# A two-turn hardware loop and its register waits written out as constants, on five engines of one core

## The chip, the cores and the metric

The kernel runs on one core of a Trainium2 chip. The metric is the device time of one execution in microseconds (us); the median of several runs is compared. Engines are named as in the profile: PE is TensorE's matmuls (PEld its weight loads), DVE is VectorE, ACT is ScalarE, POOL is GpSimd, SP is SyncE, which only issues DMAs here. "SPq", "DVEq" and the like are what an engine's sequencer does by itself.

## The reference

The input x has 2048 tokens of 128 values. A recurrent mixer comes first, then a transformer of two layers with local attention over windows of 64 tokens.

```python
x = x + _layernorm(mixer(_layernorm(x)))                 # gated scan over the 2048 tokens
x = x + _layernorm(ffn(_layernorm(x)))                   # ffn: two of the layers below, B, N = (2, 1024)

def _layer(x, ...):
    h = shift_token(x)                                   # half of the features come from the token before
    q, k, v = split(h @ wqkv, 3)                         # 8 heads of 64
    q, k = rotary_xpos(l2norm(q) * qs, l2norm(k) * ksc)
    o = local_attention(q, k, v)                         # window of 64, looks one window back
    x = x + o @ wo
    h = layernorm(shift_token(x)) * lg + lb
    a, g = split(h @ w1 + b1, 2)
    return x + (a * gelu(g)) @ w2 + b2
```

## The kernel before

Tokens are worked on in tiles of 128, four tiles to a group (`GT = 4`, `GROUPS = 4`); the two layers run one after the other over the same 16 tiles, so there are 32 tiles and `LAST = 8` groups. After the mixer each engine runs a sequence of passes. Pass `G` has four steps `j`; in step `j` the engine works on several tiles at different stages (`cur`, `prev`, `mid`, `done`, `after` are the tiles `4G + j + 3 - back`). In a pass with G >= 1 the feed-forward of group `G - 1` runs at `j = 2`, after its layer norm at `j = 1`.

There is no planner. The order on each engine is that of the program text, and engines meet by counting semaphores: `wait_ge(s, n)` holds the engine until semaphore `s` has reached `n`, and an operation's `then_inc` raises it at its end.

`passes` (L262) writes the passes -1 and 0 out with G as a Python number. Then a loop on each engine (`Fori`) runs G = 1 and 2 with G in a register. The passes 3 and 4, then 5 and 6, then a half pass 7 and `ending` are written out again. Inside the loop a semaphore value such as `32 * G` is computed in registers, and so are some addresses: the DMAs of `tables`, `head_scales` and `group_in` on SP and the columns of `low_half` on POOL. SP has one more loop (L418), over the groups 1 and 2 of the mixer's result.

`settle` (L237) raises a semaphore that nobody waits for. It stands behind certain waits, in passes that are written out as well: in `variances` (DVE, L1164 and L1168), `norm_roots` (POOL, L504), behind `h2_ready` (POOL, L540), before the carry copy (POOL, L561), in `scores` (PE, L697), in `mix_values` (PE, L722) and twice in `feed_forward` (PE, L756 and L761); on SP (L235) only behind waits on a register.

What the steps below speak of, by line: `act_t_lo` (L1140, `split_inputs`, once a pass at `j = 0`) follows ScalarE's `act_t_hi` (L888) and TensorE's transposes of `h_tok` (L641). L541, L542, L505, L507 and L552 are POOL's work for one tile (rotary sums, roots of the norms, scaling); L494 scales the tables of the next group. `low_half` (L482) is done by POOL in the loop's two turns, after the tile of `j = 2`; it prepares half of the second layer's weights each time. L590 to L594 project q, k and v, L701 and L708 make the scores, L726 mixes the values. `y` (L1236) is the group's result and the copy of `x_early` (L1229) follows it on DVE. `variances` is called 12 times: for `h2` in the passes 1 to 7 and once in `ending`, for `y` in the passes 5 and 6 and twice in `ending`. It consists of four `bn_stats` (L1166), a wait for them, and four `bn_aggr` (L1170). L1034 is the same `bn_aggr` in the mixer phase, where no `settle` stands before it.

Of the kernel before, what the change touches and what calls it, by code (L numbers as in the profile page):

```python
# [24 lines left out]
GT = 4  # L25
# [10 lines left out]


CHAIN = {0: 5, 1: 6}
# [29 lines left out]
def sandwich_kernel(nc, x, w_hg_t, w_out_t, wqkv, wo, ln_g, ln_b, w1, b1, w2, b2,  # L68
                    tables, head_scales, consts, out):
    ctx = ExitStack()  # L70
    with ctx:
# [13 lines left out]
        def group_tiles(ap, g):  # L85

            return ap[:, GT * g:GT * g + GT, :] if isinstance(g, int) else ap[:, bass.ds(GT * g, GT), :]
# [137 lines left out]
        settled = {e.name: sem(f"settled_{e.name}") for e in (mybir.EngineType.SP, mybir.EngineType.DVE, mybir.EngineType.Pool, mybir.EngineType.PE)}  # L225
# [15 lines left out]

        class At:

            def __init__(self, G, j, back, layer):
# [3 lines left out]
                if isinstance(self.t, int):  # L252
                    self.valid = 0 <= self.t < DEPTH * TILES
                    self.layer = self.t // TILES
                    self.first = self.t % TILES == 0
                else:
                    self.valid, self.layer, self.first = True, layer, False

        def tile(t):
            return At(t // GT, t % GT, 3, DEPTH - 1)  # L260

        def passes(eng, body, ending, steps=None):  # L262

            body(-1, 0)
            body(0, 0)
            for layer in range(DEPTH - 1):
                G0, G1 = GROUPS * layer + 1, GROUPS * (layer + 1) - 1
                if steps:
                    steps.enter()
                with eng.Fori(G0, G1) as G:  # L270
                    if steps:
                        steps.at(G - G0, CHAIN[layer])
                    body(G, layer)
                if steps:
                    steps.leave(G1 - G0)
                body(G1, layer)
                body(G1 + 1, layer)
            for G in range(GROUPS * (DEPTH - 1) + 1, LAST - 1):
                body(G, DEPTH - 1)
            body(LAST - 1, DEPTH - 1, 2)  # L280
            ending()

        class Steps:


            def __init__(self, eng, s):
                self.eng, self.sem, self.base, self.n = eng, s, 0, 0
# [5 lines left out]
            def catch_up(self):  # L293

                self.eng.wait_ge(self.sem, self.base + self.n)
# [4 lines left out]

            def enter(self):
                self.start, self.n = self.base + self.n, 0

            def at(self, i, each):
                self.base, self.each = self.start + i * each, each

            def leave(self, times):
                assert self.n == self.each, f"a pass of the loop has {self.n} steps"
                self.base, self.n = self.start + times * self.each, 0
# [9 lines left out]
        def _(sp):  # L319
# [35 lines left out]
            def load_tables(G):  # L355
# [3 lines left out]
                sp.dma_start(head_scale[:, :], head_scales[G:G + 1].broadcast_to([P, TABW]) if isinstance(G, int)  # L359
                             else head_scales[bass.ds(G, 1), :].broadcast_to([P, TABW])).then_inc(tab_in, 16)  # L360
# [6 lines left out]
            def load_h2(F):  # L367
# [3 lines left out]
                if isinstance(F, int) and F == LAST - 1:  # L371
# [10 lines left out]
            def load_carry(F):  # L382

                need(sp, h2_in, 64 * (F + 1))
                ends = isinstance(F, int) and F % GROUPS == GROUPS - 1
                last = zeros[P - 1:P, 64:128] if ends else x_attn[P - 1:P, GT, 64:128]
                dst = x_last if isinstance(F, int) and F == LAST - 2 else x_attn
                sp.dma_start(dst[P - 1:P, 0, 64:128], last).then_inc(carry_in, 16)

            def store(F, layer):  # L390
                if layer == 0:
# [3 lines left out]
                    if not (isinstance(F, int) and F == GROUPS - 1):  # L395
# [4 lines left out]
                if not (isinstance(F, int) and F == LAST - 1):  # L400
                    need(sp, carry_in, 16 * (F + 1))


            def store_mixed(g):
                sp.dma_start(tiles_of(group_in[g, 1:1 + GTOK, :]), group_tiles(normed, g)).then_inc(xf_stored, 16)
                if not (isinstance(g, int) and g == GROUPS - 1):
# [18 lines left out]
            def body(G, layer, count=GT):  # L425
                number = isinstance(G, int)
                for j in range(count):
                    cur = At(G, j, 0, layer)
                    if j == 0 and not (number and not 0 <= G < LAST - 1):
                        load_tables(G + 1)  # L430

                        if layer == 0 or (number and G <= GROUPS):
# [4 lines left out]
                    ffn = j == 0 and not (number and G < 1)  # L437
                    if ffn:
                        load_h2(G - 1)
                    if cur.valid and not (number and cur.t < GT):  # L440
# [9 lines left out]
                    if j == 3 and number and G > GROUPS + 1:  # L450
                        store(G - 2, DEPTH - 1)
                if count == GT and not (number and (G < 1 or G > GROUPS)):
                    store(G - 1, (G - 1) // GROUPS if number else layer)
# [7 lines left out]
            passes(sp, body, ending)  # L461
# [908 lines left out]
```

## Time and profile before

| | us |
|---|---|
| runs | 435.87, 436.12, 433.83; median 435.87 |
| span of the profiled execution, from the first to the last instruction | 431.7 |
| median of the runs less that span | 4.2 |
| PE busy | 351.5 (81% of the span) |
| DVE busy | 321.6 (74%) |
| POOL busy | 301.1 (70%) |
| PEld busy | 287.5 (67%) |
| ACT busy | 280.8 (65%) |

The profile is one execution. The profiled execution's own time is not given apart from its span; the median stands for it. Busy times of one engine's instructions overlap somewhat, as they are pipelined, and the ends of matmuls are modelled. The mean granted TensorE clock is 0.941 of full speed.

### The profile page before, as it was taken

To read this page: it belongs to the slowest core of one execution; us is meant where nothing else is said; L and a number is where in the kernel's file an instruction comes from. 1 tells how busy PE (TensorE), PEld (TensorE's weight loads), DVE (VectorE), ACT (ScalarE), POOL (GpSimd) and SP (SyncE) were. 2 spreads that over 40 slices of the span, in tenths; PEclk is the share of its full clock that TensorE was granted. 3 is DMA by queue.
4 is the path that set the end of the run, shared out by engine and by line. 5 is a ranking of instruction groups with operands and counts; after the bars stand their busy time and mean duration, and the time that the engine had idled before them with its cause. 6 is when DMAs were issued, how large, how long until landed. Compare 5 with 4: busy or idle time off the path is not lost.

```text
span 431.7 us, 11030 instructions
## 1 busy us (share of the span) xinstructions
PE 351.5 (81%) x3832; PEld 287.5 (67%) x3832; DVE 321.6 (74%) x751; ACT 280.8 (65%) x844; POOL 301.1 (70%) x247
## 2 busy tenths in 40 slices
PE   1573055899999899999999999999999989988781
PEld 1352034677778687778777887788778867766561
DVE  6889964787689767966796788688869877954653
ACT  3552263688678677867786788678777868764430
POOL 2200419899999889988998699869887988780222
PEclk9996557999999999999999999999999999998966
DMA  7700042412142125112511342043204220220110
GB/s 262 225 0 0 13 125 60 110 27 50 46 118 56 32 55 141 30 30 64 133 32 33 105 94 51 15 121 76 62 3 117 65 53 2 57 57 2 24 49 25
DMA packets 42373, 28.29 MB, mean 66 GB/s; under 512 B 21668, under 2 KB 36566, under 8 KB 42326
## 3 DMA queue, kind: packets, MB, share of 16 engines
q1 hardware_dynamic: 42325, 27.68, 24.4%
q8 instruction: 27, 0.44, 0.4%
q14 instruction: 21, 0.16, 0.1%
HBM read 13.51 MB, written 3.15 MB: 39 GB/s over the span
## 4 chain that ended last, share of the span: by engine, by line
PE 37%; DVE 23%; POOL 19%; issue 11%; ACT 7%; DMA 1%; SPq 1%; POOLq 1%; DVEq 0%; ACTq 0%
POOL rn L507 7%; PE bank L726 5%; POOL rot L552 4%; PE bank L771 4%; DVE rot_sin L1153 4%; PE upper L708 3%; DVE rot_cos L1153 3%; POOL rot L541 3%; ACT probs L902 3%; PE bank L650 2%; PE bank L763 2%; DVE normed L1052 2%; PE upper L659 2%; PE bank L590 2%; DVE neg_max L1201 2%
## 5 line engine op out<-in xcount | busy, mean ns | idle before, releaser
L902 ACT ACTIVATE probs<-upper,neg_max 128x128 f32<-128x128 f32 x256 | 90.4, 369 | 48.5 <-DVE neg_max L1201 48.4
L507 POOL TENSOR_TENSOR rn<-floored,minus_half 128x16 f32<-128x16 f32 x32 | 93.8, 2930 | 2.7
L541 POOL TENSOR_TENSOR rot<-rot_cos,rot_sin 128x512 f32<-128x512 f32 x32 | 40.9, 1277 | 44.3 <-issue 23.6
L1201 DVE TENSOR_REDUCE neg_max<-upper 128x4 f32<-128x512 f32 x64 | 43.1, 684 | 27.5 <-PE upper L708 27.4
L552 POOL TENSOR_TENSOR rot<-rot,rn 128x1024 f32<-128x1024 f32 x32 | 60.9, 1903 | 2.5
L902 ACT ACTIVATION_READ_ACCUMULATOR probs<-upper,neg_max 128x1 f32 x256 | 53.0, 207 | 0.0
L590 PE MATMUL bank<-wqkv_hi,act_t_hi 128*128 128x512 f32 x96 | 43.3, 452 | 7.9 <-DVE act_t_lo L1140 2.8
L1153 DVE TENSOR_TENSOR rot_cos<-bank,tab 128x512 f32<-128x512 f32 x64 | 43.6, 681 | 2.0 <-PE bank L594 1.9
L1153 DVE TENSOR_TENSOR rot_sin<-bank,tab 128x512 f32<-128x512 f32 x64 | 43.4, 679 | 0.0
L542 POOL TENSOR_TENSOR rot<-rot_cos,rot_sin 128x512 f32<-128x512 f32 x32 | 40.9, 1279 | 0.0
L1160 DVE TENSOR_REDUCE ss<-sq 128x16 f32<-128x1024 f32 x32 | 38.7, 1209 | 2.4 <-ACT sq L944 2.3
L681 PE MATMUL upper<-const,probs 128*128 128x128 f32 x256 | 34.6, 275 | 5.4 <-ACT probs L902 5.3
L944 ACT ACTIVATE sq<-bank 128x512 f32<-128x512 f32 x64 | 36.9, 614 | 3.2 <-DVE rot_sin L1153 3.2
L591 PE MATMUL bank<-wqkv_hi,act_t_lo 128*128 128x512 f32 x96 | 38.6, 402 | 0.0
L594 PE MATMUL bank<-wqkv_lo,act_t_hi 128*128 128x512 f32 x96 | 38.6, 402 | 0.0
L726 PE MATMUL bank<-v_mid,probs_t 128*64 128x64 f32 x512 | 37.5, 228 | 0.9 <-ACT probs_t L909 0.6
L726 PEld LDWEIGHTS bank<-v_mid,probs_t 128*64 128x64 f32 x512 | 33.0, 140 | 7.0 <-issue 4.8
L726 PE MATMUL bank<-v_tok,probs_t 128*64 128x64 f32 x512 | 37.5, 228 | 0.0
L687 PEld LDWEIGHTS upper<-wo_sb,o_t 128*128 128x128 f32 x256 | 33.5, 193 | 3.4 <-ACT o_t L914 0.6
L687 PE MATMUL upper<-wo_sb,o_t 128*128 128x128 f32 x256 | 34.2, 277 | 0.2 <-ACT o_t L914 0.2
L708 PE MATMUL upper<-k_t,q_t 64*64 64x128 f32 x1024 | 34.3, 274 | 0.0
L590 PEld LDWEIGHTS bank<-wqkv_hi,act_t_hi 128*128 128x128 f32 x96 | 18.5, 192 | 23.1 <-issue 18.0
(140 smaller groups left out, 863.7 us busy)
## 6 DMA issues: line engine op xcount, KB each, us to landing
v_mid<-v_tok SPq DMA_DIRECT2D x64, 128.0 KB, 2.3
tab_raw<-tables SPq DMA_DIRECT2D x8, 512.0 KB, 3.4
h_tok<-group_in SPq DMA_DIRECT2D x14, 128.0 KB, 3.5
x_res<-group_in SPq DMA_DIRECT2D x28, 64.0 KB, 1.8
wqkv_raw<-wqkv SPq DMA_DIRECT2D x2, 768.0 KB, 6.8
x_in<-x SPq DMA_DIRECT2D x4, 256.0 KB, 3.6
head_scale<-head_scales SPq DMA_DIRECT2D x8, 128.0 KB, 4.0
group_in<-normed SPq DMA_DIRECT2D x4, 256.0 KB
```

Source lines behind the costliest of these rows:

```text
L507: pool.tensor_tensor(rn[:, 0:2 * HEADS], floored[:, 0:2 * HEADS], minus_half[:, :], ALU.pow).then_inc(rn_ready, 1)
L541: pool.tensor_tensor(rot[cur.par][:, :, 0:32], rot_cos[:, :, 0:32], rot_sin[:, :, 32:64], ALU.add).then_inc(rot_added, 1)
L542: pool.tensor_tensor(rot[cur.par][:, :, 32:64], rot_cos[:, :, 32:64], rot_sin[:, :, 0:32], ALU.add).then_inc(rot_added, 1)
L552: pool.tensor_tensor(rot[cur.par][:, :, :], rot[cur.par][:, :, :], rn[:, 0:2 * HEADS].unsqueeze(2).broadcast_to([P, 2 * HEADS, DH]), ALU.m ...
L590: pe.matmul(out_ap, lhs, rhs, start=True, stop=False)
L687: last = pe.matmul(to[:, 0:DIM], o_t[:, c, :], wo_sb[a.layer][:, c, :], start=(c == 0), stop=(c == 3))
L708: last = pe.matmul(s_bank[half][low:low + 64, p * P:(p + 1) * P], q_t[rows, p, low:low + 64], k_t[rows, p, at:at + P], start=False, stop=T ...
L726: last = pe.matmul(o_bank[low:low + 64, cols], probs_t[:, h, low:low + 64], v[:, cols], start=True, stop=True)
L902: last = act.activation(probs[:, h, :], s_bank[half][:, (h % 4) * P:(h % 4 + 1) * P], ACT.Exp, bias=neg_max[a.par][:, h:h + 1], accum_out= ...
L1153: dve.tensor_tensor(dst[:, n * HEADS:(n + 1) * HEADS, :], src, table.unsqueeze(1).broadcast_to([P, HEADS, DH]), ALU.mult).then_inc(done, 1)
L1160: dve.tensor_reduce(ss[:, :], sq[:, :].rearrange("p (h d) -> p h d", h=2 * HEADS), AX.X, ALU.add).then_inc(ss_ready, 1)
L1201: dve.tensor_reduce(neg_max[a.par][:, 4 * half:4 * half + 4], src, AX.X, ALU.max, negate=True).then_inc(max_ready, 1)
```

## The change

All passes from -1 to 6 and the half pass 7 are written out with G as a number, so the loop, the registers, the loop's own chain count (`Steps.enter`, `at`, `leave`) and every `isinstance` branch go. Every `settle` goes, with its semaphores. SP's loop over the mixer's groups is written out. `low_half` is done where G is 1 or 2. No operation, transfer, buffer or order is changed otherwise.

```diff
-        settled = {e.name: sem(f"settled_{e.name}") for e in (mybir.EngineType.SP, mybir.EngineType.DVE, mybir.EngineType.Pool, mybir.EngineType.PE)}
         def need(eng, s, value):
-            if isinstance(value, int) and value <= 0:
-                return
-            eng.wait_ge(s, value)
-            if eng.engine == mybir.EngineType.SP and not isinstance(value, int):
-                settle(eng)
-
-        def settle(eng):
-            eng.sem_inc(settled[eng.engine.name], 1)
+            if value > 0:
+                eng.wait_ge(s, value)
...
-        def passes(eng, body, ending, steps=None):
-            body(-1, 0)
-            body(0, 0)
-            for layer in range(DEPTH - 1):
-                G0, G1 = GROUPS * layer + 1, GROUPS * (layer + 1) - 1
-                if steps:
-                    steps.enter()
-                with eng.Fori(G0, G1) as G:
-                    if steps:
-                        steps.at(G - G0, CHAIN[layer])
-                    body(G, layer)
-                if steps:
-                    steps.leave(G1 - G0)
-                body(G1, layer)
-                body(G1 + 1, layer)
-            for G in range(GROUPS * (DEPTH - 1) + 1, LAST - 1):
-                body(G, DEPTH - 1)
-            body(LAST - 1, DEPTH - 1, 2)
+        def passes(body, ending):
+            for G in range(-1, LAST - 1):
+                body(G)
+            body(LAST - 1, 2)
             ending()
...
-            with sp.Fori(1, GROUPS - 1) as g:
-                need(sp, xf_ready, g + 1)
+            for g in range(1, GROUPS - 1):
+                sp.wait_ge(xf_ready, g + 1)
                 store_mixed(g)
...
-                    cols = bass.ds(G * n - n, n)
+                    cols = slice(G * n - n, G * n)
...
                 pool.wait_ge(ss_ready, t + 1)
-                settle(pool)
...
-                        if j == 2 and not (number and G < 1):
+                        if j == 2 and G >= 1:
                             pool.wait_ge(h2_ready, G)
-                            settle(pool)
...
-                    if not number and layer == 0 and j == 2:
+                    if G in (1, 2) and j == 2:
                         low_half(G)
...
                 need(pe, pt_saved1, a.t)
-                settle(pe)
...
                     if h == PAIRS:
                         pe.wait_ge(pt_saved1, a.t + 1)
-                        settle(pe)
...
                     if c == 0:
                         pe.wait_ge(h2_split, F + 1)
-                        settle(pe)
...
             def variances(src, done, at=0):
-                settle(dve)
                 for k in range(GT):
                     last = dve.bn_stats(stats[:, k, :], src[:, k, :])
                 link(last)
-                settle(dve)
                 for k in range(GT):
                     last = dve.bn_aggr(mean_var[:, at + k, :], stats[:, k, :])
                 last.then_inc(done, 1)
```

## Rows read from the trace of the kernel before

**Rows 1.** The page: chain of work that ended last, shares by engine.
```profile
PE 37%; DVE 23%; POOL 19%; issue 11%; ACT 7%; DMA 1%; SPq 1%; POOLq 1%; DVEq 0%; ACTq 0%
```
**Rows 2.** Table of stretches: length, busy us of each engine (instructions), clock, DMA share.
```profile
127.21:169.81 42.60, 40.08 (x479) 33.47 (x475) 32.83 (x63) 32.31 (x100) 37.84 (x30) 1.00 0.26 66
169.81:212.24 42.43, 39.83 (x474) 33.31 (x470) 32.83 (x64) 32.31 (x100) 37.66 (x30) 1.00 0.26 66
212.24:254.20 41.96, 40.07 (x481) 33.36 (x474) 32.72 (x63) 32.27 (x100) 34.76 (x28) 1.00 0.27 68
254.20:296.27 42.07, 40.08 (x482) 33.38 (x474) 32.86 (x63) 32.28 (x100) 34.99 (x28) 1.00 0.26 67
```
**Rows 3.** Timeline of VectorE: start, us, instruction, idle time before and its releaser.
```profile
161.14 0.69 DVE L1201 TENSOR_REDUCE neg_max<-upper 128x4 f32<-128x512 f32 x1 [2.04 <-PE upper L708]
...
196.12 0.69 DVE L1236 TENSOR_TENSOR y<-bank,x_attn 128x512 f32<-128x512 f32 x1 [1.35 <-PE bank L771]
196.84 0.54 DVE L1229 COPY x_attn<-x_early 128x256 f32<-128x256 f32 x1
...
238.28 0.69 DVE L1236 TENSOR_TENSOR y<-bank,x_attn 128x512 f32<-128x512 f32 x1 [1.25 <-PE bank L771]
239.01 0.29 DVE L1229 COPY x_attn<-x_early 128x256 f32<-128x256 f32 x1
...
245.75 0.69 DVE L1201 TENSOR_REDUCE neg_max<-upper 128x4 f32<-128x512 f32 x1 [1.81 <-PE upper L708]
```
**Rows 4.** Timeline of GpSimd.
```profile
195.40 1.83 POOL L482 TENSOR_TENSOR wqkv_lo<-wqkv_raw,wqkv_hi  x1
...
241.86 1.29 POOL L541 TENSOR_TENSOR rot<-rot_cos,rot_sin 128x512 f32<-128x512 f32 x1 [4.16 <-issue]
```
**Rows 5.** Chain that ended last, start, us, what: loop's second turn, then pass 3.
```profile
167.31 1.08 PE bank L726 x32
168.39 0.60 PE bank L641 x4
...
169.10 0.59 ACT act_t_hi L888
...
169.81 0.70 DVE act_t_lo L1140
...
211.00 0.59 PE bank L641 x4
```
**Rows 6.** Timelines of ScalarE and VectorE, pass 3.
```profile
211.62 0.58 ACT L888 CAST act_t_hi<-bank 128x512 fp32r<-128x512 f32 x1 [0.87 <-PE bank L641]
...
212.24 0.69 DVE L1140 TENSOR_TENSOR act_t_lo<-bank,act_t_hi 128x512 fp32r<-128x512 f32 x1 [2.15 <-ACT act_t_hi L888]
```
**Rows 7.** VectorE's groups by line: busy us, mean ns, idle us before, releaser.
```profile
L1170 DVE BATCH_NORM_AGGREGATE mean_var<-stats 128x2 f32<-128x6 f32 x48 | 4.8, 159 | 2.1 <-DVE stats L1166 1.8
...
L1034 DVE BATCH_NORM_AGGREGATE mean_var<-stats 128x2 f32<-128x6 f32 x48 | 3.7, 151 | 0.1
```
**Rows 8.** Timeline of VectorE: the first tile's sum of squares, the last `y`.
```profile
64.24 1.22 DVE L1160 TENSOR_REDUCE ss<-sq 128x16 f32<-128x1024 f32 x1 [1.60 <-ACT sq L944]
...
423.36 0.87 DVE L1166 BATCH_NORM_STATS2 stats<-y 128x6 f32<-128x128 f32 x4 [0.16 <-DVE y L1236]
```
**Rows 9.** Timeline of GpSimd, first tile.
```profile
65.67 0.25 POOL L505 TENSOR_SCALAR floored<-ss 128x16 f32<-128x16 f32 x1 [0.36 <-DVE ss L1160]
```
**Rows 10.** Chain that ended last, pass 3.
```profile
243.40 1.08 PE bank L726 x32
244.48 0.34 PE upper L701 x4
```
**Rows 11.** TensorE's groups by line.
```profile
L726 PE MATMUL bank<-v_mid,probs_t 128*64 128x64 f32 x512 | 37.5, 228 | 0.9 <-ACT probs_t L909 0.6
```
**Rows 12.** The page: DMA queue (packets, MB, share), DMA issues (KB, us to landing).
```profile
q8 instruction: 27, 0.44, 0.4%
...
v_mid<-v_tok SPq DMA_DIRECT2D x64, 128.0 KB, 2.3
```

More of the change, by code:

```diff
@@ L35 @@
 RSQRT_SEED = 0x5F3759DF
-CHAIN = {0: 5, 1: 6}
 def rotary_tables():
@@ L299, in link @@
                 self.catch_up()
[L301 to L309, printed above, removed]
         def low_pieces(l):
@@ L399, in store @@
                     sp.dma_start(by_group(out)[F - GROUPS], y_out[:, :, :]).then_inc(stored, 16)
-                if not (isinstance(F, int) and F == LAST - 1):
+                if not (F == LAST - 1):
                     need(sp, carry_in, 16 * (F + 1))
@@ L449, in body @@
                         load_carry(G - 1)
-                    if j == 3 and number and G > GROUPS + 1:
+                    if j == 3 and G > GROUPS + 1:
                         store(G - 2, DEPTH - 1)
-                if count == GT and not (number and (G < 1 or G > GROUPS)):
-                    store(G - 1, (G - 1) // GROUPS if number else layer)
+                if count == GT and 1 <= G <= GROUPS:
+                    store(G - 1, (G - 1) // GROUPS)
             def ending():
@@ L736, in feed_forward @@
             def feed_forward(F, layer, t_now, between=None):
-                taken = min(t_now, DEPTH * TILES) if isinstance(F, int) else t_now
+                taken = min(t_now, DEPTH * TILES)
                 pe.wait_ge(h2t_saved, 2 * F + 1)
@@ L780, in _, with body @@
             transpose_inputs(0)
-            def body(G, layer, count=GT):
-                number = isinstance(G, int)
-                if number and G == GROUPS - 1:
+            def body(G, count=GT):
+                if G == GROUPS - 1:
                     pe.wait_ge(w_high, 2 * DEPTH)
@@ L787, in body @@
                 for j in range(count):
-                    cur, prev, mid, done, after = (At(G, j, back, layer) for back in range(5))
-                    ffn = j == 2 and not (number and G < 1)
+                    cur, prev, mid, done, after = (At(G, j, back) for back in range(5))
+                    ffn = j == 2 and G >= 1
                     if cur.valid:
@@ L807, in body @@
                         pe.wait_ge(k_saved, prev.t + 1)
-                    if j == 0 and not (number and not 0 <= G < LAST - 1):
+                    if j == 0 and 0 <= G < LAST - 1:
                         transpose_inputs(G + 1)
@@ L814, in body @@
                     if ffn:
-                        feed_forward(G - 1, (G - 1) // GROUPS if number else layer, cur.t + 1 if not number
-                                     else min(cur.t + 1, DEPTH * TILES + 4))
+                        feed_forward(G - 1, (G - 1) // GROUPS, min(cur.t + 1, DEPTH * TILES + 4))
             def ending():
@@ L925, in gelus, with body @@
                                    bias=b1_sb[l][0:cn, 3 + c:4 + c]).then_inc(gelu_done, 1)
-            def body(G, layer, count=GT):
-                number = isinstance(G, int)
+            def body(G, count=GT):
                 for j in range(count):
-                    cur, prev, mid, done = (At(G, j, back, layer) for back in range(4))
+                    cur, prev, mid, done = (At(G, j, back) for back in range(4))
                     if mid.valid:
@@ L957, in body @@
                         save_o(done)
-                    if j == 0 and not (number and not 0 <= G < LAST - 1):
+                    if j == 0 and 0 <= G < LAST - 1:
                         save_inputs(G + 1)
-                    if j == 2 and not (number and G < 1):
+                    if j == 2 and G >= 1:
                         F = G - 1
-                        l = F // GROUPS if number else layer
+                        l = F // GROUPS
                         for dst in (h2_hi, h2_t):
@@ L1192, in add_residual @@
                 dst = x_early[:, a.slot, :] if a.slot < 2 else x_attn[:, a.slot + 1, :]
-                if isinstance(a.t, int) and a.group == LAST - 1:
+                if a.group == LAST - 1:
                     dst = x_last[:, a.slot + 1, :]
@@ L1225, in place_early @@
             def place_early(G):
-                if not (isinstance(G, int) and G >= LAST - 1):
+                if not (G >= LAST - 1):
                     dve.wait_ge(xa_ready, GT * G + 2)
@@ L1254, in normalise_out, with body @@
                 last.then_inc(y_normed, 1)
-            def body(G, layer, count=GT):
-                number = isinstance(G, int)
+            def body(G, count=GT):
                 for j in range(count):
-                    cur, prev, mid, done, after = (At(G, j, back, layer) for back in range(5))
-                    norm, ffn = (j == n and not (number and G < 1) for n in (1, 2))
-                    final = j == 3 and number and G > GROUPS
+                    cur, prev, mid, done, after = (At(G, j, back) for back in range(5))
+                    norm, ffn = (j == n and G >= 1 for n in (1, 2))
+                    final = j == 3 and G > GROUPS
                     if mid.valid and j != 3:
@@ L1286, in body @@
                         variances(y, y_var, GT)
-                    if j == 0 and not (number and not 0 <= G < LAST - 1):
+                    if j == 0 and 0 <= G < LAST - 1:
                         split_inputs(G + 1)
```

94 lines of the change are left out of this document (43 added, 51 removed).

## The prediction

> **What bounds the kernel now.** I read four views in this order. First the shares of the chain that ended last [rows 1]: no engine holds it alone. TensorE has 37%, VectorE 23%, GpSimd 19%, and DMA 1%. So a saving counts only where the engine that makes it is next on that chain, and transfers hardly matter. Second, the table of the passes, cut from one `act_t_lo` (L1140, once a pass) to the next [rows 2]. The first two rows are the two turns of the loop (G = 1, 2), the others are passes that are already written out (G = 3, 4). They are at most 0.64 us apart: 42.60 and 42.43 us against 41.96 and 42.07. This is the heart of the case: the kernel before holds its own preview, since most passes are straight-line code already, and only two turns of one loop are left to gain from. Third, the engines' instructions around the few places where a turn differs from a written-out pass [rows 3 to 6]. Fourth, the places where a `settle` increment stands in front of an operation [rows 7 to 10], since the change removes those in every pass, not only in the loop.
>
> **The loop's two turns.** Against the mean of the two written-out passes, 42.015, the turns lose 42.60 − 42.015 = 0.585 and 42.43 − 42.015 = 0.415, together 1.00 us. Not all of this is the loop's. In both turns GpSimd also does `low_half` (L482): POOL's busy time is 37.8 and 37.7 us there and 34.8 and 35.0 later [rows 2]. That work is not removed; it moves to `G in (1, 2)`, the same two passes. Where it hurts is seen on VectorE: the copy of `x_early` after `y` takes 0.54 us at 196.84, and 0.29 at 239.01, where GpSimd is idle [rows 3]; at 196.84 GpSimd is inside L482, which starts at 195.40 and takes 1.83 us [rows 4]; a second L482 instruction follows. So 0.25 us a turn, 0.50 in two, stays. I leave it in: `y` and `low_half` both move forward by a few tenths, and the copy still falls into the stretch of L482.
>
> What is left of the 1.00 is 0.50 us, and rows show what it is made of. In the turn, TensorE's `h_tok` transposes start at 168.39, ScalarE follows at 169.10, VectorE at 169.81: 0.71 and 0.71 us [rows 5]. Written out: 211.00, 211.62, 212.24, so 0.62 and 0.62 [rows 6]. Each of the two waits on a register costs about 0.09 us, when its engine has nothing else to do. The same before `y`: VectorE idles 1.35 us in the turn and 1.25 later [rows 3]. So a pass pays 0.2 to 0.3 us at three places on the chain; the many other register waits lie on engines that are ahead. The table's rows begin at the `act_t_lo` of their pass, so the pair of lags at the entry (the first j = 0 in the loop) lies ahead of the first row; it is worth 2 × 0.09 = 0.18, of which I take 0.15. Sum for the loop: 0.50 + 0.15 = 0.65 us. Bounds: 0.3 if half of the lags are absorbed elsewhere, and 1.0 + 0.18 = 1.2 if the slow copy goes too.
>
> The branch itself: a stall at the turn from G = 1 to 2 would be in the first row's 42.60, and that row exceeds the second by 0.17 us, which is the 2 × 0.09 of the lags. I price the branch at 0, with 0.1 as the other end.
>
> **The `settle` increments.** VectorE shows their price well. In the mixer phase a `bn_aggr` waits for its own `bn_stats` with nothing between: idle 0.1 us in total at L1034 over five such places. In `variances`, the same wait with a `settle` behind it has 1.8 us over 12 places, 0.15 each [rows 7]. So a `settle` that stands between a fulfilled wait and the operation costs 0.15 − 0.02 = about 0.13 us; I take 0.11. In ten of the 12 calls, the nine in the passes and the one on `y` between the last two feed-forwards, VectorE next waits for TensorE or is off the chain, and the saving goes into that wait. Two calls are on the chain: the last `h2`, where the one ahead of `bn_aggr` counts, and the last `y`, where both count, since VectorE has only just written `y` (423.36, idle 0.16) [rows 8]. That is 3 × 0.11 = 0.33 us.
>
> On GpSimd, `norm_roots` has one in front of L505 for each of 32 tiles. In the first tile GpSimd waits there: `ss` ends at 64.24 + 1.22 = 65.46 and L505 starts at 65.67 [rows 8, 9], 0.21 us late, so 0.11 is gained once. In the others `ss` was ready and GpSimd runs its instructions back to back; nothing. The `settle` after `h2_ready` (j = 2) is followed by 4.16 us of idle time on GpSimd in a written-out pass [rows 4], so it is covered by that; in the two turns its cover is `low_half`, which would only end earlier.
>
> On TensorE `scores` and `mix_values` have one each per tile, and `feed_forward` two a group: 80 in all. In `scores` it stands between L726 and L701. The 32 matmuls of L726 take 1.08 us and L701 begins as they end, 243.40 + 1.08 = 244.48 [rows 10]; L726 followed by the `h_tok` transposes, with no `settle`, takes the same 1.08, from 167.31 to 168.39 [rows 5]. So TensorE issues over it, price 0. The one behind `h2_split` may be exposed, 8 times: at VectorE's 0.11 that would be 0.9 us, the upper bound; I take 0.
>
> **The queues.** SP's own loops write out too, its `settle`s and the register-addressed DMAs of tables, `h_tok` and residuals go, and its DMAs issue some tenths earlier. Every DMA of the passes and its order stay. Nobody on the chain waits for them: TensorE's idle time before L726, which needs `v_mid`, is 0.9 us over 512 instructions and is ended by ScalarE [rows 11]. If that cover failed, the cost would be the tenths themselves. Gain 0. The loop over `store_mixed` (L418) ends earlier and only advances `v_mid` of tile 0, under the same cover.
>
> **The sum.** −0.65 − 0.33 − 0.11 = −1.09 us. The profiled execution spans 431.7 us; the median of the runs is 435.87, so 4.2 us lie around the span by that median (the three runs go from 433.83 to 436.12). Nothing in the change touches those. Span 430.6, time 435.87 − 1.09 = 434.8 us, −0.25%.
>
> **What a measurement can tell.** About 0.5%, 2.2 us, separates a difference from none here: below 433.7 is faster, above 438.1 slower.
>
> **Rivals.**
> (1) A hidden stall at the branch: the first instructions after the jump come late on every engine, but lie under waits that would end earlier without them. VectorE idles 2.04 us right behind the turn, waiting for TensorE [rows 3]. If the stall were the cause and all of it went, the time would be 434.8 − 2.04 = 432.8, faster. Against it: the same wait is 1.81 us long in a written-out pass (245.75) [rows 3], and the first turn's row leaves 0.17 us for a stall [rows 2]. Chance 0.1. Beside it stands the Trainium skill, "Runtime: NRT & Kernel Launch", section "Instruction fetch mechanics": a taken branch whose target is outside the fetched pages waits for a DMA of the target, which is why kernels are written out. By that rule the time would be this rival's 432.8, by the rows the forecast's 434.8; the trace shows no such stall.
> (2) Slower: the code of the pass that is no longer repeated has to be fetched while its engines run. The page counts 27 packets of 0.44 MB, 16 KB each, on the larger instruction queue [rows 12]. They serve the whole span less one turn that is run from code already there, so a pass has 27 × 42.6 / (431.7 − 42.6) = about three. A packet that is waited for has no row; the landing of a `v_mid` transfer, 2.3 us [rows 12], bounds it from above. Three exposed give 434.8 + 6.9 = 441.7. One alone gives 437.1, still within 0.5%; from two on it decides. Against it: G = 3 and 4 fetch as much and run at 41.96 and 42.07 with no hole. Chance 0.07.
> (3) The exposed `settle`s are more: TensorE's after `h2_split` cost 0.11 each and the slow copy goes as well. 434.8 − 0.9 − 0.5 = 433.4. For it: VectorE's price. Against it: TensorE's L726. Chance 0.13.
> (4) The lags are absorbed and nothing but the tail moves: −0.4, 435.4. Chance 0.15.
> The forecast itself (−0.6 to −1.7 us) has 0.55.
>
> **How the numbers follow.** Likeliest 434.8. Its own bounds: −(0.3 + 0.3) gives 435.3, −(1.2 + 0.44 + 0.9) gives 433.3. The medians move with the runs' spread by some 0.7 us either way. So 432.7 to 436.1 holds the forecast, (3), (4) and part of (1). Faster by over 0.5%: (1), half of (3), and a little of the forecast's lower edge with the spread, 0.2. Slower: (2), 0.07. Same: 0.73.
>
> **What the profile after would show.** The table of rows 2 cut the same way: both first passes at 42.2 to 42.3, the others unchanged at 42.0 to 42.1. The lags of rows 5 at 0.62. The copy still 0.5 us in G = 1 and 2. The idle time at L1170 down from 1.8 to under 0.6 us, the tail from the last `y` to the end shorter by 0.2. TensorE's wait for `h_lo` unchanged. Some four instruction packets more. Passes at 42.0 in G = 1 and 2 would say that the copy was the loop's; passes G = 3, 4 shorter by 0.1 that TensorE's `settle` had a price; a pass over 43 that the fetch is seen.

## The result, and the profile after

The changed kernel takes 431.94 us (median of 11 runs, 431.28 to 433.16), the kernel before 434.08 beside it (11 runs, 433.49 to 436.33). The ratio is 0.9948 with a 95% interval of 0.9927 to 0.9970. Timed a second time (the last run below) it was 431.72 by 433.07, ratio 0.9953 (0.9929 to 0.9977). So the change makes the kernel about 0.5% faster; 434.8 was forecast, with 432.7 as the lower end.

Of the miss of 2.9 us, 435.87 − 434.08 = 1.8 is the base. Two of the three runs that gave 435.87 were from an upper group (of the eleven, six lie at 433.5 to 434.1 and five at 435.9 to 436.3; what puts a run there was not found). A second profile of the kernel before has a time of its own, 433.54 us for a span of 431.8, and the changed kernel's profiled run took 431.58 for 429.8. So 1.8 us lie around the span, not 4.2, and the sum should have been made against 431.7 + 1.8 = 433.5, which no figure ahead of the result showed. The rest is the sum: 1.09 us was forecast; the medians differ by 2.1, the profiled spans by 1.9.

The page of the changed kernel: the span, two instruction queues, and the chain's shares.

```profile
span 429.8 us, 10620 instructions
...
q8 instruction: 31, 0.51, 0.5%
q14 instruction: 21, 0.17, 0.1%
...
PE 40%; DVE 21%; POOL 18%; issue 9%; ACT 7%; DMA 2%; SPq 1%; POOLq 0%; DVEq 0%; ACTq 0%
```

Against [rows 1] "issue", time in which an engine waited for nothing that the profile shows, falls from 11% to 9%. The larger instruction queue has 31 packets in place of the 27 of [rows 12]. The table of the passes, cut as in [rows 2]:

```profile
127.18:169.45 42.27, 40.14 (x481) 33.40 (x474) 32.90 (x63) 32.49 (x100) 38.01 (x30) 1.00 0.27 68
169.45:211.75 42.30, 40.12 (x482) 33.43 (x474) 32.91 (x63) 32.47 (x100) 37.72 (x30) 1.00 0.26 67
211.75:253.55 41.80, 40.12 (x482) 33.41 (x474) 32.60 (x63) 32.33 (x100) 34.75 (x28) 1.00 0.27 68
253.55:295.43 41.88, 40.12 (x482) 33.45 (x474) 32.60 (x63) 32.28 (x100) 35.01 (x28) 1.00 0.25 65
```

The first two rows do what was forecast, 42.27 and 42.30. The last two were to stay at 41.96 and 42.07, and they fall by 0.16 and 0.19, though their code has lost nothing but `settle` increments. In the passes 1 to 6 the same two things have changed where the feed-forward starts. There VectorE writes `h` (the layer norm), GpSimd waits for it and then runs its two rotary additions of j = 2, VectorE subtracts to get `h_lo` (the program's `h2_lo`, the low part of the feed-forward's input), and TensorE waits for `h_lo`. Here it is in pass 3, first before (timelines of POOL, DVE and PE; start, us, instruction, idle time before):

```profile
228.86 1.27 POOL L541 TENSOR_TENSOR rot<-rot_cos,rot_sin 128x512 f32<-128x512 f32 x1 [1.44 <-DVE h L1177]
230.09 1.27 POOL L542 TENSOR_TENSOR rot<-rot_cos,rot_sin 128x512 f32<-128x512 f32 x1
...
227.45 1.11 DVE L1177 TENSOR_SCALAR h<-h,mean_var,rn 128x128 f32<-128x128 f32 x4 [1.19 <-POOL rn L514]
...
230.86 1.05 DVE L1217 TENSOR_TENSOR h_lo<-h_t,h_hi 128x512 fp32r<-128x512 f32 x1 [1.17 <-ACT h_t L918]
...
232.06 0.47 PE L763 MATMUL bank<-h_lo,w_hi 128*128 128x512 f32 x1 [0.38 <-DVE h_lo L1217]
```

and the same rows after:

```profile
228.27 1.27 POOL L493 TENSOR_TENSOR rot<-rot_cos,rot_sin 128x512 f32<-128x512 f32 x1 [1.32 <-DVE h L1118]
229.51 1.29 POOL L494 TENSOR_TENSOR rot<-rot_cos,rot_sin 128x512 f32<-128x512 f32 x1
...
226.99 1.12 DVE L1118 TENSOR_SCALAR h<-h,mean_var,rn 128x128 f32<-128x128 f32 x4 [1.20 <-POOL rn L468]
...
230.40 0.94 DVE L1158 TENSOR_TENSOR h_lo<-h_t,h_hi 128x512 fp32r<-128x512 f32 x1 [1.17 <-ACT h_t L863]
...
231.39 0.50 PE L710 MATMUL bank<-h_lo,w_hi 128*128 128x512 f32 x1 [0.17 <-DVE h_lo L1158]
```

TensorE's matmul follows the end of `h_lo` after 231.39 − 231.34 = 0.05 us, where it took 232.06 − 231.91 = 0.15: the `settle` behind `h2_split` is gone there (both readings of a `settle` here are tried below). And `h_lo` itself takes 0.94 in place of 1.05. GpSimd's first addition starts 0.16 us after `h` ends and not 0.30 (the `settle` behind `h2_ready`), so its second addition is over earlier, at 230.80 and not at 231.36. Both times `h_lo` ends about 0.54 us after that addition.

The loop's other places and the tail, timelines of ScalarE and VectorE that answer to [rows 3, 5, 8]:

```profile
160.62 0.69 DVE L1142 TENSOR_REDUCE neg_max<-upper 128x4 f32<-128x512 f32 x1 [1.72 <-PE upper L658]
...
168.83 0.59 ACT L833 CAST act_t_hi<-bank 128x512 fp32r<-128x512 f32 x1 [0.98 <-PE bank L592]
...
169.45 0.69 DVE L1084 TENSOR_TENSOR act_t_lo<-bank,act_t_hi 128x512 fp32r<-128x512 f32 x1 [2.39 <-ACT act_t_hi L833]
...
195.44 0.69 DVE L1177 TENSOR_TENSOR y<-bank,x_attn 128x512 f32<-128x512 f32 x1 [1.25 <-PE bank L718]
196.16 0.72 DVE L1170 COPY x_attn<-x_early 128x256 f32<-128x256 f32 x1
...
421.05 0.69 DVE L1177 TENSOR_TENSOR y<-bank,normed 128x512 f32<-128x512 f32 x1 [1.25 <-PE bank L718]
421.78 0.87 DVE L1108 BATCH_NORM_STATS2 stats<-y 128x6 f32<-128x128 f32 x4
422.69 0.38 DVE L1111 BATCH_NORM_AGGREGATE mean_var<-stats 128x2 f32<-128x6 f32 x4
```

ScalarE's and VectorE's starts are 0.62 us apart, not 0.71. The wait ahead of `y` is 1.25 in the former turn too. The copy of `x_early` has become slower, 0.72 where [rows 3] have 0.54: `y` moved forward more than `low_half` did. At the end `bn_stats` and `bn_aggr` follow their predecessors after 0.04 us each, where [rows 8] have 0.16 for the first.

What the profiles differ by, in order of time: up to the first `act_t_lo` +0.43, passes −1 and 0 −0.12 and −0.34, passes 1 and 2 −0.33 and −0.13, passes 3 to 5 −0.16, −0.19 and −0.17, from there to the last `y` −0.45, and from `y` to the end −0.49 (9.20 and 8.71 us). Together −1.95. The first term and the one before the last come from stretches that differ by more than that between profiles of one kernel or of near-equal ones (below); that these two cancel is chance.

### The profile page after: what moved, and what is told of

Read it like the earlier page. It is cut to its first block, busy times and chain, and to the rows that moved or that the text cites. A ratio compares the mean times of both kernels' runs of the same rounds, so it can differ in the third digit from the quotient of the medians.

```text
span 429.8 us, 10620 instructions
## 1 busy us (share of the span) xinstructions
PE 354.2 (82%) x3832; PEld 289.7 (67%) x3832; DVE 321.2 (75%) x751; ACT 281.3 (65%) x844; POOL 301.3 (70%) x247
## 4 chain that ended last, share of the span: by engine, by line
PE 40%; DVE 21%; POOL 18%; issue 9%; ACT 7%; DMA 2%; SPq 1%; POOLq 0%; DVEq 0%; ACTq 0%
POOL rn L461 5%; PE bank L675 5%; PE upper L658 4%; DVE rot_sin L1097 4%; POOL rot L504 4%; PE bank L718 4%; DVE rot_cos L1097 3%; PE bank L601 3%; ACT probs L847 3%; PE bank L541 2%; PE bank L710 2%; POOL rot L493 2%; PE upper L610 2%; PE upper L601 2%; POOL rot L494 2%
## 5 line engine op out<-in xcount | busy, mean ns | idle before, releaser
L541 PE MATMUL bank<-wqkv_hi,act_t_hi 128*128 128x512 f32 x96 | 44.3, 461 | 7.0 <-ACT sq L888 1.8
L545 PE MATMUL bank<-wqkv_lo,act_t_hi 128*128 128x512 f32 x96 | 39.5, 412 | 0.0
```

The costliest lines, as they stand in the source:

```text
L541: pe.matmul(out_ap, lhs, rhs, start=True, stop=False)
L545: return pe.matmul(out_ap, lhs, rhs_lo, start=False, stop=True)
```

## The experiments

The diffs here show the lines that matter (... stands for the others), and the comments in them are added. Where no time is given, a run is a single execution and is read by its rows alone.

Theory A: an increment between a fulfilled wait and its operation costs about 0.1 us where its engine has nothing else to issue, and the two behind `h2_split` and `h2_ready` are what the written-out passes gained. The rivals: B, straight-line code gives it; C, the 72 other increments of TensorE; D, `h_lo` is shorter for a reason other than GpSimd's start.

**How well a profile repeats.** The kernel before, unaltered:

> The kernel before, unchanged, profiled a second time, to see what two profiles of one kernel differ by. If a pass is a fixed sequence, the rows from act_t_lo to act_t_lo repeat: 42.60, 42.43, 41.96, 42.07 and 42.03 us for G = 1 to 5 within 0.05, h_lo at 1.05 us, the gap from h_lo to TensorE's next matmul at 0.15; what moves is the start before the first pass and the tail behind y of the last but one group, by some tenths to over 2 us, since the eleven times of before fall into two clusters (433.5 to 434.1 and 435.9 to 436.3). If instead the 0.10 to 0.19 us that each written-out pass gained is noise between profiles, the passes G = 3 to 5 differ here by as much.

The five passes came out at 42.63, 42.43, 41.96, 42.06 and 42.02 us, 0.03 or less from the first profile; `h_lo` took 1.05 to 1.06, and the gap from its end to the matmul that reads it was 0.14 to 0.15. So in a pass 0.1 us is a difference. The start is not as firm: over all profiles the first `act_t_lo` came at 57.2 to 58.9 us. From the last `act_t_lo` to the end it was 90.9 to 94.4. A stretch of the tail in the profiles of before (first) and after (table of stretches, columns as in [rows 2]):

```profile
408.00:414.00 6.00, 1.99 (x7) 1.39 (x8) 3.84 (x14) 1.45 (x2) 3.36 (x4) 0.79 0.15 44
414.00:420.00 6.00, 6.00 (x21) 4.49 (x20) 2.70 (x7) 1.58 (x3) 1.28 (x1) 0.64 0.15 44
```

```profile
408.00:414.00 6.00, 2.75 (x8) 2.05 (x9) 4.15 (x15) 1.45 (x2) 2.60 (x4) 0.57 0.15 44
414.00:420.00 6.00, 6.00 (x32) 4.91 (x32) 2.95 (x6) 2.06 (x3) 1.28 (x1) 0.86 0.16 46
```

In the second row of each TensorE is busy throughout, with 21 matmuls at a mean granted clock of 0.64 and with 32 at 0.86; each is a mix of its two levels (1.2 and 2.4 GHz). A few tenths in the tail of one profile are therefore no evidence for an edit. Pass rows at clock 1.00 are, and so is the stretch from the last `y` to the end, in which TensorE has no matmul: 9.20 and 9.21 us in the two profiles of before.

**The two halves of the change.** The loop's half alone, with the increments back in their old places:

```diff
+                settle(pe)       # in scores, mix_values, and twice in feed_forward
...
+                settle(dve)      # in variances, ahead of bn_stats and of bn_aggr
...
+                settle(pool)     # in norm_roots, behind h2_ready, ahead of the carry copy
```

> The changed kernel, written out, with every settle increment that stood in front of an operation of TensorE, VectorE and GpSimd put back behind its wait (SyncE's go with its register waits and stay away): the loop's half of the change alone. Theory A (the gain in the written-out passes is the increments', those behind h2_split on TensorE and h2_ready on GpSimd above all): G = 3 to 5 back to 41.96 to 42.07, h_lo 1.05, gap to TensorE 0.15, G = 1 and 2 at about 42.45 to 42.5 with the slow copy, and a time of 0.7 to 0.9 us under before's, 433.2 to 433.4. Rival B (writing out shifts the code, the queues or GpSimd's instructions, and the increments are issued over): G = 3 to 5 stay at 41.80 to 41.88, and the time stays with the changed kernel's 431.9.

The passes:

```profile
127.48:169.87 42.39, 40.12 (x482) 33.34 (x474) 32.97 (x64) 32.43 (x100) 37.99 (x30) 1.00 0.27 67
169.87:212.24 42.37, 40.10 (x482) 33.36 (x474) 32.97 (x63) 32.44 (x100) 37.66 (x30) 1.00 0.27 67
212.24:254.19 41.95, 40.08 (x482) 33.38 (x474) 32.73 (x64) 32.32 (x100) 34.70 (x28) 1.00 0.27 67
254.19:296.22 42.03, 40.09 (x482) 33.36 (x474) 32.73 (x63) 32.29 (x100) 34.96 (x28) 1.00 0.27 67
```

Passes 3 and 4 are back at their old length, `h_lo` at 1.05 to 1.06, the gap at 0.14 to 0.15. So their gain was the increments', and rival B falls for these passes. The times don't resolve this half: 434.02 by 433.73, ratio 0.9990 (0.9959 to 1.0022). The rows do: passes 1 and 2 are 0.21 and 0.06 shorter than before, pass 0 0.35 (34.68 for 35.03 in the second profile of before). The other half, the kernel before with its loop, in which only the loop's turns keep their increments:

```diff
+            if not looping:      # looping holds only inside a Fori
+                return
             eng.sem_inc(settled[eng.engine.name], 1)
...
```

> The kernel before, with its loop and register waits, and with its settle increments kept inside the loops alone: the other half of the change, in the passes that were written out already. Theory A: G = 3 to 5 at 41.80 to 41.88 as in the changed kernel (h_lo 0.93 and gap 0.05 there, 1.05 and 0.15 in G = 1 and 2), G = 1 and 2 at 42.60 and 42.43 as before; gaps at the last y 0.04. Rival B (the gain of the written-out passes came with the whole program being straight-line): G = 3 to 5 at 41.96 to 42.07.

Passes 1 and 2 were 42.62 and 42.45, as before; 3 and 5 were 41.80 and 41.85, as after. Pass 4 was 42.20, against the expectation. In it GpSimd's addition started 0.48 us after `h` and not 0.16 (timelines of POOL and DVE):

```profile
272.16 1.28 POOL L548 TENSOR_TENSOR rot<-rot_cos,rot_sin 128x512 f32<-128x512 f32 x1 [1.63 <-DVE h L1184]
273.40 1.29 POOL L549 TENSOR_TENSOR rot<-rot_cos,rot_sin 128x512 f32<-128x512 f32 x1
...
270.57 1.11 DVE L1184 TENSOR_SCALAR h<-h,mean_var,rn 128x128 f32<-128x128 f32 x4 [1.28 <-POOL rn L521]
...
273.98 1.26 DVE L1224 TENSOR_TENSOR h_lo<-h_t,h_hi 128x512 fp32r<-128x512 f32 x1 [1.16 <-ACT h_t L925]
```

One packet of the smaller instruction queue ran between 271.6 and 272.0, just ahead of the late start. That GpSimd waited for it is possible, but was not tested. What matters is the size: GpSimd 0.32 us later, `h_lo` 1.26 for 0.94, 0.32 longer, and the pass longer by as much (42.20 by 41.88).

**Which increments.** One put back at a time, first TensorE's:

```diff
                         pe.wait_ge(h2_split, F + 1)
+                        settle(pe)
```

> The changed kernel with one increment put back, TensorE's behind the wait for h2_split, eight in all. Theory A: the gap from h_lo to the first matmul that reads it goes from 0.05 to 0.15 us, h_lo stays 0.93, each pass G = 3 to 5 grows by 0.05 to 0.10 to 41.9 to 41.95. Rival C (my priced forecast: TensorE issues over its increments): gap 0.05, passes 41.80 to 41.88 as in the changed kernel.

Timelines of VectorE and TensorE in pass 3, and the pass in the table of stretches:

```profile
229.63 0.93 DVE L1165 TENSOR_TENSOR h_lo<-h_t,h_hi 128x512 fp32r<-128x512 f32 x1 [1.17 <-ACT h_t L870]
230.71 0.47 PE L717 MATMUL bank<-h_lo,w_hi 128*128 128x512 f32 x1 [0.24 <-DVE h_lo L1165]
...
210.98:252.83 41.85, 40.11 (x481) 33.43 (x474) 32.61 (x63) 32.33 (x100) 34.73 (x28) 1.00 0.27 68
```

The gap was 0.14 to 0.16, `h_lo` 0.92 to 0.93, the passes 3 to 5 41.85, 41.93 and 41.91: each 0.05 longer. So the increment costs 0.095 us where it stands, and half of that arrives; where the other half goes stays open. Four in its place:

```diff
                         pe.wait_ge(h2_split, F + 1)
+                        settle(pe, 4)
```

> The changed kernel with four increments in a row behind TensorE's wait for h2_split, to see what one costs and how much of it arrives. Theory A: each takes the sequencer about 0.095 us, so the gap after h_lo goes from 0.05 to 0.43 (0.15 with one) and the pass, which grew by 0.05 with one, by 0.05 + 3 x 0.095 = 0.33 to about 42.15 in G = 3. Rival: the price is that of breaking the wait off from its matmul once, and further increments are free: gap 0.15 to 0.2, pass 41.85 to 41.9.

```profile
232.12 0.94 DVE L1165 TENSOR_TENSOR h_lo<-h_t,h_hi 128x512 fp32r<-128x512 f32 x1 [1.16 <-ACT h_t L870]
...
233.66 0.47 PE L717 MATMUL bank<-h_lo,w_hi 128*128 128x512 f32 x1 [0.72 <-DVE h_lo L1165]
```

The gap was 0.59 to 0.60, so each further one costs (0.60 − 0.15) / 3 = 0.15 us, more than the first; passes 3 to 5 were 42.28, 42.38 and 42.34, longer by 0.43 to 0.45 than with one, which is all of it. The rival of a price paid once fell, and the expected 0.43 was too low. GpSimd's:

```diff
                             pool.wait_ge(h2_ready, G)
+                            settle(pool)
```

> The changed kernel with one increment put back, GpSimd's behind the wait for h2_ready (j = 2), seven in all. Theory A: GpSimd's addition starts 0.29 us after h ends and not 0.17, its later work meets h_lo in another place, h_lo takes 1.05 us and not 0.93, and each pass grows by about 0.1 to 41.9 to 42.0 while the gap to TensorE stays 0.05. Rival D (h_lo is shorter for another reason, the code's or ScalarE's): GpSimd starts 0.12 later, h_lo stays 0.93, passes unchanged.

Timelines of POOL, DVE and PE in pass 3, and the pass in the table of stretches:

```profile
228.83 1.27 POOL L500 TENSOR_TENSOR rot<-rot_cos,rot_sin 128x512 f32<-128x512 f32 x1 [1.44 <-DVE h L1125]
230.06 1.27 POOL L501 TENSOR_TENSOR rot<-rot_cos,rot_sin 128x512 f32<-128x512 f32 x1
...
230.84 1.05 DVE L1165 TENSOR_TENSOR h_lo<-h_t,h_hi 128x512 fp32r<-128x512 f32 x1 [1.17 <-ACT h_t L870]
...
231.94 0.50 PE L717 MATMUL bank<-h_lo,w_hi 128*128 128x512 f32 x1 [0.29 <-DVE h_lo L1165]
...
212.19:254.11 41.92, 40.12 (x482) 33.43 (x474) 32.71 (x63) 32.32 (x100) 34.74 (x28) 1.00 0.27 67
```

GpSimd starts 0.29 after `h`, `h_lo` is long again, and TensorE's gap stays 0.05. Passes 3 to 5 were 41.92, 41.99 and 42.00, longer by 0.12, 0.11 and 0.14; rival D falls. An increment on GpSimd lengthened an instruction of VectorE, for which TensorE waits. All the other increments together:

```diff
+                settle(pe)       # in scores, mix_values, behind the second half of h2t_saved
+                settle(dve)      # in variances, both
+                settle(pool)     # in norm_roots, ahead of the carry copy
```

> The changed kernel with all increments put back but the two tried alone: TensorE's in scores, mix_values and behind the second half of h2t_saved, VectorE's two in variances, GpSimd's in norm_roots and ahead of the carry. Theory A: none of them is next on the chain in a pass, so G = 3 to 5 stay at 41.80 to 41.88 within 0.04, h_lo 0.93, gap to TensorE 0.05; only the ends move: at the last y the gaps to bn_stats and from there to bn_aggr go from 0.04 to 0.15 us each, the first tile's GpSimd instruction starts 0.1 later. Rival C (TensorE's 72 others have a price that is spread over the pass): G = 3 to 5 longer by 0.1 or more.

Passes 3 to 5: 41.77, 41.87 and 41.85. They cost a pass nothing, so rival C falls, and 0.05 + 0.12 of the two alone is about the 0.15 to 0.19 that all of them cost. At the end, from the last `y` on, it was 8.93 us where the changed kernel has 8.71: VectorE's two increments at 0.11 each.

**GpSimd beside VectorE.** If `h_lo` stands still until GpSimd's second addition is over, moving that addition behind it must give back more than the increment took (the scaling of the table, which came after the addition, then goes ahead of it):

```diff
+                        if aside:                        # j == 2 and G >= 1
+                            if G < LAST - 1:
+                                scale_table(G + 1, j)
+                            pool.wait_ge(h2_split, G)
                         pool.tensor_tensor(rot[cur.par][:, :, 32:64], ...)
...
+                    if 0 <= G < LAST - 1 and not (j == 2 and G >= 1):
                         scale_table(G + 1, j)
```

> The changed kernel with GpSimd's order in j = 2 changed: the first rotary addition, then the scaling of the table, then a wait for h2_split, and only then the second addition, which so no longer runs beside h_lo. Theory A' (h_lo can't proceed while that addition runs: in the traces it ends 0.54 us after the addition's end, at 230.80 + 0.54 = 231.34 in the changed kernel and 231.36 + 0.54 = 231.90 before; that is how GpSimd's increment came to lengthen it): h_lo 0.69, passes G = 3 to 5 shorter by 0.2 to 0.25, at 41.55 to 41.65. In G = 1 and 2 GpSimd then reaches low_half 0.4 us later, so that the copy of x_early waits longer for it, 1.1 to 1.3 us, and those passes are 0.2 to 0.4 longer, not shorter. Time: five passes by -0.22, two by +0.3: about -0.5, 431.4 where the changed kernel has 431.9. Rival D' (h_lo is slowed in proportion by whatever GpSimd runs beside it): the scaling of the table, which now ends as h_lo begins, is gone too, so h_lo is also near 0.69; but then with the addition's place as before and only the table moved it would be short as well, and h_lo in the increment's run would not have followed the addition's end by a constant.

VectorE and GpSimd in pass 3:

```profile
230.53 0.69 DVE L1163 TENSOR_TENSOR h_lo<-h_t,h_hi 128x512 fp32r<-128x512 f32 x1 [1.17 <-ACT h_t L868]
...
229.63 0.72 POOL L449 TENSOR_TENSOR tab<-tab_raw,head_scale 128x256 f32<-128x256 f32 x1
231.31 1.29 POOL L499 TENSOR_TENSOR rot<-rot_cos,rot_sin 128x512 f32<-128x512 f32 x1 [0.95 <-DVE h_lo L1163]
```

`h_lo` took 0.69 in every pass, and passes 3 to 5 41.53, 41.62 and 41.61, 0.25 to 0.27 less. In passes 1 and 2 GpSimd came to `low_half` later, the copy waited 1.49 us for it, and they took 42.77 and 42.81, 0.5 longer and not 0.2 to 0.4. Pass 6 lost 0.5 too (8.26 us from `h_lo` to `y` for 7.72), for a reason not followed up. By these rows the passes gain 0.8 us and lose some 1.5. The time was 432.00, 0.9967 of before (0.9944 to 0.9991), no gain over the changed kernel and not the 0.5 us less that was expected. So `low_half` next, behind a wait for the copy:

```diff
                 pool.wait_ge(w_high, 4)
+                pool.wait_ge(early_moved, G + 1)
```

> The changed kernel with one wait more: GpSimd's low_half in G = 1 and 2 waits until VectorE has copied x_early (early_moved), and so runs in the 4 us in which GpSimd is idle. Theory A' (VectorE's copy stands until GpSimd's instruction beside it ends): the copy takes 0.29 us in G = 1 and 2 and not 0.70, both passes are shorter by about 0.4 and stand at 41.85 like the later ones; together -0.8 us, 431.1 where the changed kernel has 431.9. Rival: what the first two passes lack is not the copy, and low_half behind it delays the additions of j = 3: passes at 42.2 to 42.4 as in the changed kernel.

The copy took 0.29, but the passes 42.12 and 42.11 and not 41.85; the time was 430.55 us (6 runs), 0.9937 of before (0.9918 to 0.9956). The timeline of GpSimd in pass 2, and the same addition one pass on:

```profile
197.74 0.92 POOL L438 TENSOR_TENSOR w_lo<-w_raw,w_hi 128x341 fp32r<-128x341 f32 x1
198.61 1.27 POOL L494 TENSOR_TENSOR rot<-rot_cos,rot_sin 128x512 f32<-128x512 f32 x1
...
240.39 1.27 POOL L494 TENSOR_TENSOR rot<-rot_cos,rot_sin 128x512 f32<-128x512 f32 x1 [4.08 <-issue]
```

The addition of j = 3 comes 198.61 − 194.78 = 3.83 us after the start of `y`, and 240.39 − 236.83 = 3.56 in pass 3: GpSimd is 0.27 late, and works back to back from there on. The gain was handed to GpSimd. With the short half ahead of the copy and the long one behind it:

```diff
-                for lo, raw, hi, n in ((wqkv_lo[1], ...), (w1_lo[1], ...)):
+                for lo, raw, hi, n in ((w1_lo[1], ...), (wqkv_lo[1], ...)):
+                    if lo is wqkv_lo[1]:
+                        pool.wait_ge(early_moved, G + 1)
```

> The changed kernel with low_half's two subtractions in the other order, the short one (0.92 us) ahead of the copy of x_early and the long one (1.83 us) behind a wait for it. Behind the copy both ended 0.25 us after the place at which GpSimd's additions of j = 3 could start, and the passes G = 1 and 2 kept 0.3 of what the copy had cost. Theory A': GpSimd is done in time, the copy stays 0.29, and G = 1 and 2 fall to 41.8 to 41.9, the length of the later passes. Rival: they stay at 42.1, so something else is longer there.

The two passes took 41.81 and 41.85, as long as a pass without `low_half`. That settles the last 0.45 us of the first two passes. The run took 428.79 us, but it has the shortest tail of all the profiles (90.9). Both moves at once:

> Both moves on the changed kernel: the second addition of j = 2 behind h_lo, and low_half's short half ahead of the copy, its long half behind it. Theory A': h_lo 0.69, G = 3 to 5 at 41.53 to 41.62 as with the first move alone. GpSimd reaches low_half some 0.7 us later than without the first move, so that its short half is beside the copy, which takes 0.6 to 0.8 us; G = 1 and 2 at 41.7 to 41.9. Against the changed kernel 6 x 0.26 + 2 x 0.2 = 2.0 us less, about 430 by 431.9, and about -0.9% to before. Rival: what is saved ahead of y is lost behind it to GpSimd, which works back to back over the turn of the group: G = 3 to 5 no shorter than 41.8.

```profile
126.86:168.76 41.90, 40.06 (x482) 33.40 (x474) 32.59 (x64) 32.32 (x100) 37.58 (x30) 1.00 0.27 68
168.76:210.64 41.88, 40.03 (x481) 33.42 (x474) 32.58 (x64) 32.32 (x100) 37.27 (x30) 1.00 0.27 67
210.64:252.15 41.51, 40.05 (x481) 33.43 (x474) 32.35 (x64) 32.32 (x100) 34.31 (x28) 1.00 0.27 68
```

Pass 3 is as short as with the first move alone, and the first two are about as short as the later passes of the changed kernel. Pass 6 keeps its loss (8.26 us from `h_lo` to `y`). Time 429.31 us (6 runs), 0.9893 of before (0.9851 to 0.9934). The changed kernel beside it, once more:

> The changed kernel once more, unaltered, timed beside the kernel with both moves and the kernel before on one chip. Passes as in the first profile within 0.05: 42.27, 42.30, 41.80, 41.88, 41.86. What differs lies in the start (57.3 to 58.5 us to the first act_t_lo in the profiles so far) and the tail (91.5 to 94.3 us behind the last). Time about 2 us under before's median: 1.96 us from the rows up to G = 6 and the tail, if the median of before falls where it fell in the first comparison, 1.2 to 2.8 if not.

It took 431.72, ratio 0.9953, with passes of 42.28, 42.28, 41.77, 41.87 and 41.86. The version with both moves is 2.4 us below it and 3.8 below before.

## Why the prediction was wrong

**The base** was the median of three runs; the eleven have 434.08. This alone put the time outside the stated range: 432.7 to 436.1, moved down by 1.8, is 430.9 to 434.3 and holds 431.94. The gain is another matter. 1.09 us was forecast and 2.1 came, and for that terms of the sum failed.

**"The settle after h2_ready is followed by 4.16 us of idle time, so it is covered"** is the step that failed in the sum. [Rows 4] show that idle time ahead of the addition at 241.86, which is the next tile's, j = 3. The increment stands ahead of the addition of j = 2, at 228.86, and there GpSimd is next: it has waited for `h`. The price taken as 0 was 0.11 to 0.14 us in each of the passes 3 to 5; in 1, 2 and 6 `h_lo` was as much longer. The increment doesn't work by being on the chain itself, but by moving an instruction that blocks VectorE's `h_lo`.

**TensorE's `h2_split` at 0**, the other mis-sized term: 0.095 where it stands and 0.05 a pass. The bound of 0.11 held, and the value taken was too low. It was judged by `scores` [rows 10], where TensorE had work to issue over; behind `h2_split` it stands idle until `h_lo` is there. For the 72 others, 0 was right.

Together the two account, within the 0.03 us by which a pass repeats, for the 0.52 us in passes 3 to 5 and for the 0.07 to 0.12 by which passes 1 and 2 of the changed kernel are shorter than with the increments. Of rival (3), the price of TensorE's increment came true at half the size, and the slow copy did not go.

**The loop, 0.65**, was right in sum by luck and wrong in its parts. Without the increments' share it gave 0.21 and 0.06 in the two turns and 0.35 in pass 0, of which 0.24 came at the entry's `act_t_lo` (VectorE's wait ahead of it fell from 2.09 to 1.85), where I had 0.15. The lag of [rows 5] from ScalarE to VectorE is 0.62 us now, as forecast. The turns gave 0.27 and not 0.50, partly because the copy grew (0.54 to 0.65 in that run): I had kept its price constant, though it ends when GpSimd's instruction does.

**VectorE's increments** at the last `y`: two gaps of 0.16 and 0.15 [rows 7, 8] became 0.04 each, 0.23 us, as priced; the third, at the last `h2`, lies in a stretch of the tail that the clock blurs. Another 0.24 came from the last four `bn_aggr`, before:

```profile
424.38 0.62 DVE L1170 BATCH_NORM_AGGREGATE mean_var<-stats 128x2 f32<-128x6 f32 x4 [0.15 <-DVE stats L1166]
```

They took 0.62 us in both profiles of before, where the fourth starts late (424.82), and 0.38 in the run with the increments back and in the one with the loop kept. Either half of the change alone was enough to remove it, so it belongs neither to the loop nor to the increments as such; its cause stays open, and no term of the sum had it. The first tile's start on GpSimd came 0.24 after its idle time began and not 0.36 [rows 9], as priced.

**Rival (1)**, the stall at the branch: VectorE's wait of 2.04 us behind the turn [rows 3] became 1.72, not zero, and the written-out run with its increments gained 0.21 and 0.06 in the turns. TensorE works right across the turn: its scores start at 159.94, take 1.04, and the second turn's first projection starts at 161.01. Leaving the loop, where nothing jumps, the same two starts are 202.55 and 203.52, so jump and register waits together cost TensorE 0.1 us. The rule of the Trainium skill, "Runtime: NRT & Kernel Launch", section "Instruction fetch mechanics", says that a taken branch to a target outside the fetched pages waits for its code. The trace has no stall at the jump of the size that this rival put on it, 2.04 us. Whether the target lay outside the fetched pages, which is the rule's condition, no run here shows. **Rival (2)**: four packets more, as counted, and no hole in the changed kernel's passes; the one late start above, 0.32 us in another kernel, is a seventh of the 2.3 us of the bound, if it was a packet's at all.

## What to carry to other kernels

An increment between a fulfilled wait and its operation cost 0.1 to 0.15 us on three engines wherever the engine had nothing else to issue, and nothing measurable where it had, so price such work place by place, and check with the timeline that the idle time you cover it with is ahead of the same instruction. When an engine off the chain moves, look at what its instruction blocks on the other engines, not only at who waits for its result. Set a sum that is read from a profile against that profile's own time, not against the median of three runs.

## What the runs showed of the hardware

`h_lo` (two inputs in SBUF) alone takes 0.69 us. Beside GpSimd's addition it ends 0.54 to 0.56 us after that addition's end, whether GpSimd started 0.16, 0.29 or 0.48 us after `h`. The two overlapped by 0.40, 0.50 and 0.71 us, and each time the same 0.55 was left at the addition's end; slowed in proportion, `h_lo` would have had less left the longer the overlap. GpSimd's next instruction, the scaling of the table, then takes 1.18 us and not 0.72. The copy of `x_early` ends about 0.15 us after GpSimd's `low_half` instruction: 196.88 for 196.74 after, 197.38 for 197.23 in [rows 3, 4]. `y`, which reads PSUM, kept its 0.69 us beside that same instruction. This is waiting, not sharing. The Trainium skill, "SBUF — State Buffer", section "SBUF: two separate sides", describes a port pair that GpSimd, or VectorE in a two-port mode or with two SBUF inputs, holds alone for a whole instruction. The traces agree for `h_lo`, by the constant 0.55 us; which mode the copy ran in they don't show.
